# Two PSUM banks for the down projections, two for the side results, and a shifted schedule of side work

## What is computed

```python
x = x + attn_a(layernorm(x))   # 16 heads, each the difference of two softmax attentions, RMS norm, projection
x = x + ffn(layernorm(x))      # 64 experts, top 8 of each token, and one shared expert
x = x + attn_b(layernorm(x))   # 16x16 attention between heads, its energy summed over all tokens of a batch
x = x + ffn(layernorm(x))      # the same experts again
```

```python
aff = xf @ centroids.T
_, idx = jax.lax.top_k(aff + expert_biases, 8)
w = jax.nn.sigmoid(jnp.take_along_axis(aff, idx, axis=1))
w = w / (jnp.sum(w, axis=-1, keepdims=True) + 1e-08)          # scattered into cw, zero elsewhere
h = jax.nn.silu(jnp.einsum('td,edf->etf', xf, W_up))
y = jnp.einsum('etf,efd->etd', h, W_down)
routed = jnp.einsum('etd,te->td', y, cw)                       # plus silu(xf @ Ws_up) @ Ws_down
```

## Time and profile before

| | us |
|---|---|
| median of 3 runs | 1110.72 (1108.67 to 1111.96) |
| the profiled execution, its own time | 1112.18 |
| its span, first to last instruction | 1110.4 |
| PE busy in the span | 1013.9 (91%) |
| DVE busy | 963.0 (87%) |
| ACT busy | 891.8 (80%) |
| POOL busy | 515.6 (46%) |
| mean granted TensorE clock | 0.97 of full |

### The profile page before, as it was taken

One profiled execution on the slowest core, in us unless ns is written; L12 is line 12 of the kernel. 1 busy time (PEld: TensorE's weight loads), 2 busy tenths in 40 slices (PEclk: granted clock), 3 DMA queues, 4 the chain that ended last, 5 costly groups with the idle time before them and its releaser, 6 DMA issues.

```text
span 1110.4 us, 21656 instructions
## 1 busy us (share of the span) xinstructions
PE 1013.9 (91%) x8016; PEld 517.5 (47%) x8016; DVE 963.0 (87%) x1174; ACT 891.8 (80%) x1466; POOL 515.6 (46%) x905
## 2 busy tenths in 40 slices
PE   6389999999999999999999999998899889999997
PEld 3022222222222223232322337776678667777875
DVE  7799999999999999999999738888868986687665
ACT  5189999999999999999999868767576767677765
POOL 3353556455645554455446645364325441442332
PEclk9579999999999999999999979999999999999999
DMA  8911110011001110111010026755567465857773
GB/s 279 302 33 36 51 49 24 29 51 50 25 27 51 50 31 22 51 50 31 23 51 21 3 68 166 175 135 135 143 155 187 114 171 138 209 142 176 190 194 86
DMA packets 80473, 108.91 MB, mean 98 GB/s; under 512 B 23536, under 2 KB 33520, under 8 KB 80368
## 3 DMA queue, kind: packets, MB, share of 16 engines
q1 hardware_dynamic: 70752, 103.07, 35.0%
q10 hardware_dynamic: 9616, 4.46, 1.5%
HBM read 95.57 MB, written 11.93 MB: 97 GB/s over the span
## 4 chain that ended last, share of the span: by engine, by line
DVE 57%; PE 22%; ACT 7%; issue 6%; DMA 5%; POOL 2%; SPq 1%; ACTq 0%; DVEq 0%; POOLq 0%
DVE NEGMAX L1057 46%; PE PS L1449 6%; PE PS L1451 5%; PE PS L1450 5%; DVE HF L1098 3%; DVE XC L1004 3%; DMA GATE<-gate_d 2%; PE PS L1351 2%; DVE HL L1106 2%; ACT HH L941 2%; PE PS L1324 1%; ACT PR L863 1%; ACT PS L948 1%; DVE ln_st L992 1%; DMA shift_d<-SHT 1%
## 5 line engine op out<-in xcount | busy, mean ns | idle before, releaser
L1057 DVE TENSOR_REDUCE NEGMAX<-PS 128x1 f32<-128x1024 f32 x512 | 585.0, 1211 | 9.7 <-PE PS L1287 9.1
L863 ACT ACTIVATE PR<-PS 128x512 f32<-128x512 f32 x1024 | 539.5, 601 | 42.4 <-PE PS L1324 30.3
L1351 PE MATMUL PS<-PR,VG 128*32 128x256 f32 (+1 forms) x3840 | 324.8, 410 | 16.7 <-ACT PR L863 1.3
L1324 PE MATMUL PS<-QB,KB 32*128 32x512 bf16 x1024 | 261.4, 390 | 3.7 <-DMA QB<-shift_d 2.3
L1287 PE MATMUL PS<-KA,QA 32*128 32x512 bf16 x1024 | 204.6, 397 | 30.3 <-DVE NEGMAX L1057 22.6
L1098 DVE TENSOR_TENSOR HF<-PS,GATE 128x1024 f32<-128x1024 f32 x128 | 156.1, 1221 | 71.0 <-ACT PS L948 70.6
L948 ACT ACTIVATE PS<-PS 128x1024 f32<-128x1024 f32 x128 | 129.3, 1010 | 91.7 <-PE PS L1451 90.5
L1324 PEld LDWEIGHTS PS<-QB,KB 32*128 32x128 bf16 x1024 | 75.2, 91 | 242.4 <-ACT PR L863 140.5
L775 POOL TENSOR_TENSOR HL<-HF,HH 128x1024 fp32r<-128x1024 f32 (+1 forms) x44 | 99.1, 2254 | 169.9 <-ACT HH L941 169.6
L941 ACT ACTIVATE HH<-HF 128x1024 fp32r<-128x1024 f32 (+1 forms) x136 | 139.7, 1028 | 26.9 <-DVE HF L1098 25.6
L1351 PEld LDWEIGHTS PS<-PR,VG 128*32 128x32 f32 x3840 | 76.7, 108 | 131.5 <-issue 65.9
(11 more groups left out here) (187 smaller groups left out, 991.4 us busy)
## 6 DMA issues: line engine op xcount, KB each, us to landing
GATE<-gate_d SPq DMA_DIRECT2D x256, 256.0 KB, 4.1
QA<-q_stack SPq DMA_DIRECT2D x64, 128.0 KB, 2.6
QB<-q_stack SPq DMA_DIRECT2D x16, 256.0 KB, 3.0
KB<-k_stack SPq DMA_DIRECT2D x16, 256.0 KB, 3.0
KA<-k_stack SPq DMA_DIRECT2D x60, 64.0 KB, 2.4
q_stack<-PARTS SPq DMA_DIRECT2D x12, 256.0 KB, 4.4
k_stack<-PARTS SPq DMA_DIRECT2D x12, 256.0 KB, 4.5
RAWU<-in_L_ffn_W_up_dram ACTq DMA_DIRECT2D x4, 512.0 KB, 13.3
```

What stands on the lines that cost most here:

```text
L863: nc.scalar.activation(PR[:, s % PRING, r, :], PS[:, SCORE_BANK[n], :], ACT.Exp, scale=SCALE_A).then_inc(p_ready, 1)
L1057: nc.vector.tensor_reduce(NEGMAX[:, hs % 2, col:col + 1], PS[:, e:e + 2, :].rearrange("p b n -> p (b n)"), axis=AX_X, op=ALU.max, negate=T ...
L1324: mm(PS[:, SCORE_BANK[n], :], KB[strip, u, mt * P:(mt + 1) * P], QB[strip, u, half * BANK:(half + 1) * BANK], start=True, stop=True).then_ ...
L1351: last = mm(PS[STRIP * r:STRIP * (r + 1), 7, cols], VG[:, u, mt, r // 2, :], PR[:, s % PRING, r, cols], start=mt == 0, stop=mt == TB - 1 a ...
```

## The change

- `gate_T` of chunk 0 moves from quad NQ - 4 to NQ - 2. For feed-forward chunk 3, `x_T` moves from (1, 16) to (2, 0), `affinity` from (2, 0) to (2, 1), `top`, `sum` and `gate_T` by one step each. In chunks 2 and 4 the `x_T` of the second attention and all that follows it move by one step, `v_all` of the second half into (n + 1, 0).
- The write of VP and the read of RT are issued by ScalarE, as items of (n + 1, 0) and (n + 1, 2), and no longer by SyncE.
- `low_on_pool`: steps with an `affinity` go to GpSimd, the last five subtractions to VectorE.
- Side results use banks 6 and 7; down projections of even chunks bank 4, of odd chunks bank 5.
- ScalarE takes the `affinity` item (copy and sigmoid) behind the step's silu instead of ahead of it.

```diff
--- before.py
+++ after.py
@@ -153,7 +153,7 @@
 SIDE = {
 
     NQ - 12: [("heads_T", 0)], NQ - 11: [("proj", 0), ("stats", ("f", 0))], NQ - 10: [("norm", ("f", 0))],
-    NQ - 8: [("x_T", ("f", 0))], NQ - 7: [("affinity", 0)], NQ - 6: [("top", 0)], NQ - 5: [("sum", 0)], NQ - 4: [("gate_T", 0)],
+    NQ - 8: [("x_T", ("f", 0))], NQ - 7: [("affinity", 0)], NQ - 6: [("top", 0)], NQ - 5: [("sum", 0)], NQ - 2: [("gate_T", 0)],
 
     (0, 2): [("heads_T", 1)], (0, 4): [("proj", 1), ("stats", ("f", 1))], (0, 6): [("norm", ("f", 1))],
     (0, 8): [("x_T", ("f", 1))], (0, 9): [("affinity", 1)], (0, 11): [("top", 1)], (0, 13): [("sum", 1)],
@@ -161,8 +161,8 @@
     (1, 2): [("heads_T", 2)], (1, 4): [("proj", 2), ("stats", ("f", 2))], (1, 5): [("y_T", 0), ("stats", ("b", 0))],
     (1, 6): [("norm", ("f", 2))], (1, 7): [("norm", ("b", 0))], (1, 8): [("x_T", ("f", 2))], (1, 9): [("affinity", 2)],
     (1, 10): [("heads_T", 3), ("x_T", ("b", 0))], (1, 11): [("top", 2)], (1, 12): [("proj", 3), ("stats", ("f", 3))],
-    (1, 13): [("sum", 2)], (1, 14): [("norm", ("f", 3))], (1, 15): [("gate_T", 2)], (1, 16): [("x_T", ("f", 3))],
-    (2, 0): [("affinity", 3)], (2, 2): [("top", 3)], (2, 4): [("sum", 3)], (2, 6): [("gate_T", 3)],
+    (1, 13): [("sum", 2)], (1, 14): [("norm", ("f", 3))], (1, 15): [("gate_T", 2)],
+    (2, 0): [("x_T", ("f", 3))], (2, 1): [("affinity", 3)], (2, 3): [("top", 3)], (2, 5): [("sum", 3)], (2, 7): [("gate_T", 3)],
     (4, 1): [("top", 5)], (4, 3): [("sum", 5)], (4, 5): [("gate_T", 5)],
     (6, 1): [("top", 7)], (6, 3): [("sum", 7)], (6, 5): [("gate_T", 7)], (6, 7): [("y_T", 5)],
     (7, 5): [("y_T", 6)],
@@ -179,16 +179,17 @@
     c, f = 2 * b + 1, 2 * b + NCH
     also((n, 4), ("y_T", n - 1), ("stats", ("b", c)))
     also((n, 6), ("norm", ("b", c)))
-    also((n, 7), ("x_T", ("b", c)))
-    also((n, 8), ("gram", b))
-    also((n, 9), ("gram_k", b))
-    also((n, 10), ("q_k", b))
-    also((n, 11), ("energy", b))
-    also((n, 12), ("soft_exp", b), ("soft_mix", b))
-    also((n, 13), ("mix_T", b))
-    also((n, 14), ("v_mix", b))
-    also((n, 15), ("v_all", 2 * b))
-    also((n, 16), ("v_all", 2 * b + 1))
+    also((n, 8), ("x_T", ("b", c)))
+    also((n, 9), ("gram", b))
+    also((n, 10), ("gram_k", b))
+    also((n, 11), ("q_k", b))
+    also((n, 12), ("energy", b))
+    also((n, 13), ("soft_exp", b), ("soft_mix", b))
+    also((n, 14), ("mix_T", b))
+    also((n, 15), ("v_mix", b))
+    also((n, 16), ("v_all", 2 * b))
+    also((n + 1, 0), ("v_all", 2 * b + 1), ("mix_out", b))
+    also((n + 1, 2), ("mix_back", b))
     also((n + 1, 4), ("y_T", n))
     also((n + 1, 5), ("out_b", 2 * b), ("stats", ("f", f)))
     also((n + 1, 6), ("out_b", 2 * b + 1), ("stats", ("f", f + 1)))
@@ -232,8 +233,12 @@
 
 def low_on_pool(g):
 
-    n, w = divmod(g + 1, WIDES)
-    return g >= POOL_BUSY and (works((n, w), DVE_SIDE) and not works((n, w), POOL_SIDE) or not works((n, w), POOL_SIDE) and w % 3 == 0)
+    here = divmod(g + 1, WIDES)
+    if not POOL_BUSY <= g < 2 * NCH * WIDES - 5:
+        return False
+    if works(here, ("affinity",)):
+        return True
+    return not works(here, POOL_SIDE) and (works(here, DVE_SIDE) or here[1] % 3 == 0)
 
 
 def lows_before(g, pool):
@@ -266,20 +271,19 @@
 
 
 SCORE_BANK, TILE_BEFORE = score_banks()
-TAIL_BANK, SIDE_BANKS = 1, (5, 6, 7)
-DOWN_BANK = 4
+TAIL_BANK, SIDE_BANKS, DOWN_BANKS = 1, (6, 7), (4, 5)
 
 
 def side_bank(item):
 
     n = SIDE_ITEM[item]
-    return TAIL_BANK if n < TAIL_ITEMS else SIDE_BANKS[n % 3]
+    return TAIL_BANK if n < TAIL_ITEMS else SIDE_BANKS[n % 2]
 
 
 def bank_before(item):
 
     n = SIDE_ITEM[item]
-    return SIDE_ORDER[n - 1] if 0 < n <= TAIL_ITEMS else SIDE_ORDER[n - 3] if n >= TAIL_ITEMS + 3 else None
+    return SIDE_ORDER[n - 1] if 0 < n <= TAIL_ITEMS else SIDE_ORDER[n - 2] if n >= TAIL_ITEMS + 2 else None
 
 
 
@@ -547,16 +551,6 @@
 
             rows_out = out.rearrange("b (n p) c -> p (b n) c", p=P)
 
-            def mix_out(b):
-                sp.wait_ge(*evacuated(("v_all", 2 * b + 1)))
-                sp.dma_start(mixed_d[b].rearrange("i d a j -> (d a) i j"), VP[:]).then_inc(mix_w[b], 16)
-
-            def mix_back(b):
-                sp.wait_ge(mix_w[b], 16)
-                if b:
-                    sp.wait_ge(*evacuated(("out_b", 1)))
-                sp.dma_start(RT[:], mixed_d[b].rearrange("i d a j -> (i d) (a j)")).then_inc(mix_r[b], 16)
-
             def store(c):
                 sp.wait_ge(*evacuated(("y_T", NCH + c)))
                 sp.dma_start(rows_out[:, 4 * c:4 * c + 4, :], X[:, 4 * c:4 * c + 4, :]).then_inc(stored, 16)
@@ -576,10 +570,6 @@
                     for h in range(2):
                         sp.dma_start(GATE[E * h:E * (h + 1), k % GSLOTS, :, :],
                                      gates[w, h].partition_broadcast(E)).then_inc(gate_ld[k % GSLOTS], 16)
-                    if (n, w) in ((3, 1), (5, 1)):
-                        mix_out((n - 3) // 2)
-                    if (n, w) in ((3, 3), (5, 3)):
-                        mix_back((n - 3) // 2)
                     if n > NCH and w == 9:
                         store(n - NCH - 1)
                 if n < 2 * NCH - 1:
@@ -887,11 +877,13 @@
                 act.wait_ge(side_full, SIDE_ITEM[item] + 1)
                 nc.scalar.activation(dst, src, func).then_inc(side_act, 1)
 
-            def side(where):
+            def side(where, routing=False):
 
                 for item in SIDE.get(where, ()):
                     stage, arg = item
                     bank = side_bank(item) if item in SIDE_ITEM else None
+                    if routing != (stage == "affinity" and item not in TAIL_SIDE):
+                        continue
                     if item in TAIL_SIDE:
                         if stage == "affinity":
                             act.wait_ge(*evacuated(item))
@@ -928,6 +920,14 @@
                             act.wait_ge(mix_w[0], 16)
                         side_evac(item, VP[:, :, h * (S1 // 2):(h + 1) * (S1 // 2)],
                                   PS[:, bank, :].rearrange("p (j i) -> p i j", i=S0))
+                    elif stage == "mix_out":
+                        act.wait_ge(*evacuated(("v_all", 2 * arg + 1)))
+                        act.dma_start(mixed_d[arg].rearrange("i d a j -> (d a) i j"), VP[:]).then_inc(mix_w[arg], 16)
+                    elif stage == "mix_back":
+                        act.wait_ge(mix_w[arg], 16)
+                        if arg:
+                            act.wait_ge(*evacuated(("out_b", 1)))
+                        act.dma_start(RT[:], mixed_d[arg].rearrange("i d a j -> (i d) (a j)")).then_inc(mix_r[arg], 16)
 
             def high(g):
 
@@ -955,7 +955,7 @@
 
             def chunk_sum(n):
                 act.wait_ge(down_ok, (n + 1) * WIDES)
-                nc.scalar.activation(YS[:], PS[:, DOWN_BANK, :], ACT.Copy).then_inc(y_evac, 1)
+                nc.scalar.activation(YS[:], PS[:, DOWN_BANKS[n % 2], :], ACT.Copy).then_inc(y_evac, 1)
 
             for s in range(NQ):
                 exp_quad(s)
@@ -969,6 +969,7 @@
                 side((n, w))
                 if g > 1:
                     silu(g)
+                side((n, w), True)
                 if g:
                     high(g - 1)
             high(2 * NCH * WIDES - 1)
@@ -1470,8 +1471,8 @@
 
                 n, w = divmod(g, WIDES)
                 k = g % HPLACES
-                if w == 0 and n:
-                    pe.wait_ge(y_evac, n)
+                if w == 0 and n >= 2:
+                    pe.wait_ge(y_evac, n - 1)
                 pe.wait_ge(hh_ok, g + 1)
                 if low_on_pool(g):
                     pe.wait_ge(hl_pool, lows_before(g + 1, True))
@@ -1480,7 +1481,7 @@
                 for u in range(2 if w < FULL else 1):
                     j = 2 * w + u
                     wh, wl = (WDH[:, j * DIM:(j + 1) * DIM], WDL[:, j * DIM:(j + 1) * DIM]) if w < FULL else (WSDH[:], WSDL[:])
-                    last = split3(PS[:, DOWN_BANK, :], wh, wl, HH[:, k, u, :], HL[:, k, u, :], j == 0, w == FULL)
+                    last = split3(PS[:, DOWN_BANKS[n % 2], :], wh, wl, HH[:, k, u, :], HL[:, k, u, :], j == 0, w == FULL)
                 last.then_inc(down_ok, 1)
 
             for s in range(-LEAD, NQ):
```

## The result

The changed kernel takes 1104.87 us (median of 5 runs, 1104.20 to 1106.63) where the kernel before takes 1110.72 us (median of 5, 1108.67 to 1111.96). The ratio is 0.9944, with a 95% interval of 0.9927 to 0.9961: faster by 5.9 us, where 10.2 were forecast. It was measured again as an experiment, in ten runs: 1106.83 us, ratio 0.9961 (0.9946 to 0.9976). The profiled execution has a span of 1104.3 us against 1110.4.

What follows compares the result with a forecast made beforehand. TensorE was taken to set the pace where side work is little, VectorE where norms and top-8 picks fall; terms -4.0 - 3.2 - 2.1 - 1.7 + 1.8 - 1.0 = -10.2 took 1110.7 to 1100.5 us, range 1095.5 to 1107.5.

Steps and rivals of the forecast that it cites:

- gate transpose: End of attention, chunk 0: moving it two quads later removes TensorE's wait and half clock; -4.0 us (-1.7 to -5).
- down projections in two banks: Chunk starts: first down matmul no longer waits for ScalarE's copy of the old sum; -3.2 us (-2.2 to -4.4).
- transposes, chunk 4: Second batch-attention inputs transposed one step later, so TensorE waits less for the norm; -2.1 us (0 to -3.8).
- transposes and routing, chunk 2: Same move in chunk 2, with the third chunk's transposes, affinity and top-8 also later; -1.7 us (+1 to -3.7).
- affinities outside chunk 2: Affinity behind the silu, subtraction on GpSimd: +1.0 each in chunks 0 and 1, -0.2 in chunk 3; +1.8 us (-2 to +6).
- side banks, exchange and chain: Two side-result banks and the DRAM exchange on ScalarE's queue: 0 (to +1) each; items behind the transposes meet no wait.
- last subtractions: Kernel's end: on VectorE instead of GpSimd they let down matmuls start 1.1 us earlier; -1.0 us (-0.5 to -1.3).
- the new idle at the front: Rival, chance 0.12: TensorE's stand before the first product costs a clock fall of 1.7 or 6.8 us; 1102.2 to 1107.3.
- a fall of the clock in new places: Sign that the prediction is wrong: TensorE's clock falls in places where it does not in the kernel before.
- a wait of over 1.5 us for GpSimd's subtraction: Sign that the prediction is wrong: at affinity steps GpSimd's subtractions hold down matmuls over 1.5 us each.
- Meet no wait: Chunks 2 and 4: items behind the moved transposes move along without a wait, their chain having 2.9 us per link.
- the slower rival: Rival, chance 0.05: in seven affinity steps `high`, GpSimd's subtraction and the next silu pile up; +21 us, 1121.

## Why the prediction was right in sign and too large by 4.4 us

The measured 1104.87 us lies within the stated range, 1095.5 to 1107.5. Term by term, from the step starts of the two profiles; the measured column adds up to -6.2, where the spans differ by -6.1.

| term | forecast | measured | from |
|---|---|---|---|
| gate transpose | -4.0 | -4.3 | first product 663.13 to 658.81 |
| given back in chunk 0 by (0, 9) | | +0.5 | side work, as far as seen |
| down projections in two banks | -3.2 | -3.5 | -0.76, -0.72, -0.27, -0.73, -0.25, -0.73 |
| transposes, chunk 4 | -2.1 | -2.3 | (4, 6) to (4, 9) |
| transposes and routing, chunk 2 | -1.7 | -1.5 | (1, 13) to (2, 9) |
| affinities outside chunk 2 | +1.8 | +2.5 | +0.9, +0.7, -0.4, +0.3, +0.6, +0.4 |
| half-clock stretches at 737 and 976 | | +2.4 | 20.21 - 18.95 and 15.65 - 14.50 |
| side banks, exchange and chain | 0 | +1.9 | (2, 9) to (3, 1), (4, 9) to (5, 1) |
| last subtractions | -1.0 | -1.0 | down of (7, 14) |
| end | | -0.9 | last transfer lands sooner |

- **Gate.** The step was right, with its next limit: the product waits 2.52 us for the gate's load and starts at 658.81, forecast 658.8 to 659.2. What I took as fixed is not: the half clock behind the stall was long in two profiles and short in a third, and alone the move gave 2.6 us in the medians and 3.65 in the step starts. A fall of the clock behind the new idle at the front did occur, in the second profile of the changed kernel and with the gate alone, though not in the first profile. It cost nothing by (0, 9), where that rival had 1.7 us.
- **Banks.** Right in size, and hidden in chunk 2 as said; undone, it cost 3.5 us in the medians and 3.2 in the step starts.
- **Transposes.** Right where it was worked out from the norm and the product behind it. The experiment that undid both found 5.9 us, with half-clock stretches behind the returned waits.
- **Affinities.** This term was too small. The two silus stand 5.3 us apart, as reckoned, and TensorE waits for the slow subtraction, also as reckoned. Outside chunk 2 the part cost 2.5 us in place of 1.8, and in chunk 2, (2, 1) to (2, 6), another 1.0, which stands in the row of chunk 2: 17.94 us with it and 16.91 without. The failed part is the sentence that chunk 5 and the ends of chunks 3 and 5 lose nothing: against the kernel with the part undone they lose 0.6, 0.45 and 0.45 us, as 16.14 against 15.69 from (4, 1) to (4, 6). The old order used ScalarE's idle time while it waited for the product behind a long norm: in (5, 10) the copy began at 982.40, 1.0 us behind the start of a `high` that had waited 2.90. The new order puts the same 3.4 us where ScalarE has none to spare. Undoing the part gave 4.1 us in the medians. Its two halves do not add: the order costs in either case, the subtraction on GpSimd costs about 3 us with the old order (1103.71 against 1100.75) and nothing with the new one (1106.83 against 1108.29).
- **Half clock.** The largest loss that no term had is 2.4 us at (1, 9) and (5, 10): there two short stretches cost 1.3 and 1.2 us in the first profile, and such stretches cost nothing with the old order. The forecast named a fall of the clock in new places as a sign of being wrong, and one did fall where none was before (737); another sign, a wait of over 1.5 us for GpSimd's subtraction, shows once, 1.73 us in chunk 2.
- **The chain.** "Meet no wait" was wrong by 0.9 us a batch. Moving it by one step against a rule that goes by w % 3 put VectorE's subtraction, 1.22 us, ahead of the copy of `mix_T`. Giving that subtraction back to GpSimd removed the wait for MIX and brought that for MIXT back to 0.50 us, 0.74 of the 0.9 in all. What holds the last 0.2 is open; ScalarE as the issuer of the two transfers was not tried apart.
- **The end.** 0.9 us came that no term had, since the last transfer landed sooner behind its issue; that was luck.
- **Rivals.** None came about as a whole. The largest loss of both kernels, which the change does not touch, is the norm under GpSimd's subtractions: its group has 37.1 us of busy time with them over it and 18.8 without. The Trainium skill's rule on the port pair (SBUF — State Buffer, "SBUF: two separate sides") had been used as the slower rival's reason only. It holds under a condition that the prediction left out: the VectorE instruction must be in a two-port mode or have two inputs in SBUF. The trace agrees as far as it goes: the norm, from SBUF to SBUF, was held; the product, with one input in PSUM, kept 1.22 us. Which mode the norm ran in no row shows.

## What to carry to other kernels

Before moving an item behind the critical instruction, look whether its old place lay in idle time of its engine: work that filled a wait costs little there, may hide a stretch of half clock as well, and can cost its full length in the new place. An instruction of VectorE that takes three or five times its usual time in a timeline may be held rather than busy: see what GpSimd runs over it. Keeping that out of the steps with norms paid here, though VectorE must then do the work itself. A step schedule and a rule that assigns engines by step number must be moved together.

## What the runs showed of the hardware

- Four `tensor_scalar` instructions of 128 x 128 from SBUF to SBUF took 1.1 us alone, 3.2 us with one GpSimd subtraction of 128 x 1024 over them and 5.1 us with two. The product of PSUM and SBUF (128 x 1024) kept its 1.22 us beside GpSimd's subtraction.
- The granted clock fell to 0.50 around or behind stalls of TensorE of 1.2 to 3.9 us, but not behind each: it stayed at 1.00 behind one of 3.51 us in the kernel before (at 915 us). The same kernel had such stretches of 3.4 us at three places in one execution and at five in another, and a stall of 1.70 us was followed by 13.6 us of it in two profiles and by 3.4 us in a third. A stretch of 3.4 us cost from nothing (old order, (5, 10)) to 1.6 us (second profile of the changed kernel, at 768 and at 802). In ten runs of one kernel the mean granted clock went from 0.970 to 0.979 and the time from 1109.73 to 1104.17 us.
